# A decoder layer pair on one Trainium2 core: the last step of the norms on GpSimd, the expert tiles' PSUM copies on ScalarE, the last batch's gathers issued together

## What is computed

```
layer 0:  x = norm(x + decay_scan(x) @ o_w.T)             norm 0
          x = norm(x + cross_attention(x, ctx))           norm 1
          x = norm(x + fp4_gated_mlp(x))                  norm 2
layer 1:  h = norm(x) * gamma + beta                      norm 3
          a = x + linear_attention(h) @ wo
          h = norm(a) * gamma + beta                      norm 4
          x = norm(gelu(gelu(h @ w1 + b1) @ w2 + b2) + a + x)   norm 5
          x = norm(x + cross_attention(x, ctx))           norm 6
          x = norm(x + sum over 2 of 8 experts of gate * expert(x))
```

## Time and profile before

| what | value |
|---|---|
| median of 3 runs (lowest to highest) | 1092.96 us (1092.56 to 1093.59) |
| profiled execution, its own time | 1095.46 us |
| profiled execution, span of its instructions | 1093.6 us |
| busy: PE, DVE, ACT, POOL | 931.4, 681.5, 404.2, 253.5 us |
| mean granted clock of PE over the span | 0.917 |

### The profile page before, as it was taken

The page is one execution under the profiler, slowest core; times in us unless marked ns, Lnnn a source line. Parts: engine busy times, 40 slices in busy tenths (PEclk is TensorE's granted clock), DMA queues, the critical chain, the costliest instruction groups (busy, mean ns, idle before and its releaser), DMA issues.

```text
span 1093.6 us, 19946 instructions
## 1 busy us (share of the span) xinstructions
PE 931.4 (85%) x7490; PEld 734.6 (67%) x7490; DVE 681.5 (62%) x1995; ACT 404.2 (37%) x965; POOL 253.5 (23%) x384
## 2 busy tenths in 40 slices
PE   6579899888879999888999999989999997478940
PEld 4455578665655777666867887868778886367940
DVE  6997962559687543888785465784875365533124
ACT  2354334342532334433533544435343443112310
POOL 5410320115212210251221111340121112321025
PEclk9696999888888999988999999999999998599975
DMA  9996000000000000013210213314211031599912
GB/s 329 372 328 205 1 11 20 11 21 30 11 1 1 10 21 11 26 35 122 88 63 25 83 29 128 122 50 149 98 63 51 24 102 54 196 326 320 359 61 86
DMA packets 40734, 110.51 MB, mean 101 GB/s; under 512 B 5464, under 2 KB 25568, under 8 KB 39904
## 3 DMA queue, kind: packets, MB, share of 16 engines
q1 hardware_dynamic: 37568, 100.85, 27.2%
q0 software_dynamic: 3072, 8.39, 2.4%
HBM read 96.90 MB, written 35.13 MB: 121 GB/s over the span
## 4 chain that ended last, share of the span: by engine, by line
PE 60%; DVE 22%; issue 5%; DMA 5%; ACT 4%; POOL 2%; SPq 0%; POOLq 0%; DVEq 0%; ACTq 0%
PE ps L624 42%; PE ps L629 7%; PE ps L636 6%; DMA G<-ys_d,back_idx 3%; PE ps L700 2%; DVE PT L1021 2%; DVE stat L954 1%; ACT PT L1344 1%; DMA EW<-ys_d,back_idx 1%; PE ps L767 1%; DVE PT L974 1%; DVE sm L970 1%; DVE PT L979 1%; DVE X L1269 1%; POOL mv L1496 1%
## 5 line engine op out<-in xcount | busy, mean ns | idle before, releaser
L1496 POOL TENSOR_TENSOR stat<-stat,mhalf 128x1 f32<-128x1 f32 x112 | 66.2, 591 | 453.8 <-DVE stat L956 453.8
L624 PE MATMUL ps<-wall,XT 128*128 128x256 f32 (+1 forms) x448 | 137.2, 434 | 9.4 <-ACT XT L1311 4.3
L624 PEld LDWEIGHTS ps<-wall,XT 128*128 128x128 f32 x448 | 82.0, 199 | 36.5 <-issue 18.3
L636 PE MATMUL ps<-KB 32*128 32x128 f32 (+1 forms) x2048 | 81.1, 297 | 20.7 <-ACT PT L1344 4.9
L636 PEld LDWEIGHTS ps<-KB 32*128 32x128 f32 (+1 forms) x2048 | 68.5, 198 | 39.4 <-issue 28.9
L1021 DVE TENSOR_REDUCE PT<-ps 128x8 f32<-128x1024 f32 x64 | 75.3, 1219 | 26.8 <-PE ps L636 26.8
L624 PE MATMUL ps<-wgu,XT 128*128 128x352 f32 x256 | 85.1, 487 | 0.6 <-ACT XT L1311 0.6
L629 PE MATMUL ps<-cst,PT 128*128 128x128 f32 x512 | 79.0, 295 | 7.6 <-DVE PT L1012 4.6
L624 PE MATMUL ps<-XT,wall 128*128 128x128 f32 x640 | 77.1, 276 | 1.7 <-ACT XT L1361 1.5
L624 PEld LDWEIGHTS ps<-XT,wall 128*128 128x128 f32 x640 | 74.6, 192 | 5.6 <-ACT XT L1361 2.8
L629 PEld LDWEIGHTS ps<-cst,PT 128*128 128x128 f32 x512 | 62.7, 151 | 20.6 <-issue 10.1
(11 more groups left out here) (215 smaller groups left out, 1741.6 us busy)
## 6 DMA issues: line engine op xcount, KB each, us to landing
EW<-moe_w SPq DMA_DIRECT2D x31, 514.0 KB, 3.8
EW<-moe_w SPq DMA_DIRECT2D x31, 512.0 KB
PT<-moe_w SPq DMA_DIRECT2D x12, 514.0 KB, 5.9
PT<-moe_w SPq DMA_DIRECT2D x12, 512.0 KB, 7.1
XS<-xs_d SPq DMA_DIRECT2D x35, 128.0 KB, 2.4
ys_d<-YB SPq DMA_DIRECT2D x35, 128.0 KB, 3.9
wall<-wts SPq DMA_DIRECT2D x1, 4104.0 KB, 21.4
Y<-xTg SPq DMA_DIRECT2D x16, 128.0 KB, 2.2
```

The lines of the kernel that those rows point to most:

```text
L624: last = k.e.matmul(o, a, b, start=(i == 0), stop=(i == len(pairs) - 1))
L636: last = k.e.matmul(ps[:, at, c * P:(c + 1) * P], lhsT[lane, c * P:(c + 1) * P], rhs[lane, c * P:(c + 1) * P], start=True, stop=True)
L1496: return k.e.tensor_tensor(v[:, 7:8], v[:, 8:9], mhalf[:, :], ALU.pow)
```

## The change

1. The last step of norms 0 to 6 is taken from DVE. A new `pool_apply` on POOL does the same subtraction and multiplication behind the root that POOL makes itself; it still waits on `root_ready` and raises `normed`. In the plan the step costs POOL 0.65 where it cost DVE 0.41. The finish of the join (line 1275) stays on DVE.
2. Both copies from PSUM of an expert tile are taken from DVE and put on ACT, in all 46 tiles; `dve_tiles` is gone. In the plan each costs ACT 0.37 where it cost DVE 0.43.
3. In the last batch all eight "fetch" pieces, 16 gathers, come before the first join; before, three did.

With the changed costs the plan is made anew, so the interleaving on all engines and the banks can differ.

```diff
+APPLY = 0.65
@@ plan_attention
-    yield piece(work=[*[("s", 0.5, None)] * load, ("D", 0.41, (n, "done", a))])
+    yield piece(work=[*[("s", 0.5, None)] * load, ("P", APPLY, (n, "done", a))])
@@ plan_sample (and so for every norm)
-    yield piece(work=[("D", 1.27, None), ("P", 0.66, None)])
-    yield piece(work=[("D", 0.41, None)])
+    yield piece(work=[("P", APPLY, None), ("D", 0.87, None), ("P", 0.66, None)])
+    yield piece(work=[("P", APPLY, None)])
@@ plan_tiles
-            yield piece(0.3, [xT], [("D", 0.43, xT)], [("rows", x)], True)
+            yield piece(0.3, [xT], [("A", 0.37, xT)], [("rows", x)], True)
...
-            yield piece(1.78, [y], [("D", 0.43, y)],
+            yield piece(1.78, [y], [("A", 0.37, y)],
@@ join_turns
-        first = 3 if samples is BATCHES[-1] else 1
+        first = len(samples) if samples is BATCHES[-1] else 1
@@ dve_norm is gone, and its calls; dve_tiles is gone
@@ act_tiles
+                if what == "turn":
+                    act_copy(k, M["xT", x], XST[x % 2][:, :, :])
+                elif what == "down":
+                    u, i, y = M["y", x], home["store", x], user["store", x]
+                    k.wait_ge(filled[u.at], u.full)
+                    if y is not None:
+                        k.wait_ge(ys_stored[i], count["store", y])
+                    k.e.copy(YB[i][:, :], ps[:, u.at, 0:D]).then_inc(emptied[u.at], 1)
@@ pool
+        def pool_apply(k, n, ln, src, dst):
+            s = slot(n)
+            v = stat[:, s, :]
+            k.wait_ge(root_ready[s], norm_count(n, ln))
+            k.e.tensor_scalar(dst, src, v[:, 6:7], v[:, 7:8], ALU.subtract, ALU.mult).then_inc(normed[s], 1)
@@ pool_sample, pool_attention: one call behind each pool_norm, in the piece after it; for example
+            pool_apply(k, n, 2, Z[:, s, :], XB[:, s, :])
             e.memset(V1(s)[:, :, P:P + 1], 1.0)
             pool_norm(k, n, 3)
             yield
+            pool_apply(k, n, 3, XB[:, s, :], Y[:, s, :])
```

More of the change, by code:

```diff
@@ L180, in plan_sample @@
     yield piece(0.92, [(n, "o1")], [("D", 0.41, (n, "o1")), ("D", 0.87, None), ("P", 0.57, None)])
-    yield piece(work=[("p", 0.72, (n, "twice")), ("D", 0.41, None)])
+    yield piece(work=[("P", APPLY, None), ("p", 0.72, (n, "twice"))])
     load = n + NS < B
@@ L959, in dve_norm_stats @@
             dve_stats(k, stat[:, s, :], src, eps).then_inc(var_ready[s], 1)
[L961 to L965, removed]
         def dve_fp4_head(k, src, n, tmp, small, xn_sem):
@@ L984, in dve_fp4_scale, with dve_attention @@
                                      bc(small(1)[:, 0:m].unsqueeze(2), m, DH), ALU.mult)
-        def dve_attention(k, n, a, X, rope, xout):
+        def dve_attention(k, n, a, X, rope):
             e, s, u_ = k.e, slot(n), U[n]
@@ L1041, in dve_attention @@
             yield
-            dve_norm(k, n, (1, 6)[a], Z[:, s, :], xout)
             yield
@@ L1064, in dve_sample @@
             yield
-            dve_norm(k, n, 0, Z[:, s, :], XB[:, s, :])
             yield
-            yield from dve_attention(k, n, 0, XB, True, XA[:, s, :])
+            yield from dve_attention(k, n, 0, XB, True)
             k.wait_ge(normed[s], norm_count(n, 1))
@@ L1096, in dve_sample @@
             yield
-            dve_norm(k, n, 2, Z[:, s, :], XB[:, s, :])
             k.wait_ge(normed[s], norm_count(n, 2))
@@ L1100, in dve_sample @@
             yield
-            dve_norm(k, n, 3, XB[:, s, :], Y[:, s, :])
             yield
@@ L1132, in dve_sample @@
             yield
-            dve_norm(k, n, 4, XA[:, s, :], Y[:, s, :])
             yield
@@ L1146, in dve_sample @@
             yield
-            dve_norm(k, n, 5, Z[:, s, :], XA[:, s, :])
             yield
-            yield from dve_attention(k, n, 1, XA, False, X6[:, n, :])
+            yield from dve_attention(k, n, 1, XA, False)
         def dve_weights(k):
@@ L1275, in dve_join @@
                     e.tensor_scalar(x6, x6, v[:, 6:7], v[:, 7:8], ALU.subtract, ALU.mult).then_inc(out_ready, 1)
[L1276 to L1290, removed]
                 yield
@@ L1479, in act_tiles @@
             for what, x in tile_turns():
-                if what == "up":
+                if what == "turn":
[6 more added lines that the diff above has]
+                    k.e.copy(YB[i][:, :], ps[:, u.at, 0:D]).then_inc(emptied[u.at], 1)
+                elif what == "up":
                     u, i = M["h", x], home["load up", x]
@@ L1501, in pool_norm, with pool_attention @@
             pool_root(k, stat[:, s, :]).then_inc(root_ready[s], 1)
-        def pool_attention(k, n, a, X, rope):
+        def pool_apply(k, n, ln, src, dst):
[3 more added lines that the diff above has]
+            k.e.tensor_scalar(dst, src, v[:, 6:7], v[:, 7:8], ALU.subtract, ALU.mult).then_inc(normed[s], 1)
+        def pool_attention(k, n, a, X, rope, xout):
             e, s, u_ = k.e, slot(n), U[n]
@@ L1533, in pool_attention @@
             yield
+            pool_apply(k, n, (1, 6)[a], Z[:, s, :], xout)
             yield
@@ L1544, in pool_sample @@
             yield
+            pool_apply(k, n, 0, Z[:, s, :], XB[:, s, :])
             yield
-            yield from pool_attention(k, n, 0, XB, True)
+            yield from pool_attention(k, n, 0, XB, True, XA[:, s, :])
             yield
@@ L1573, in pool_sample @@
             yield
+            pool_apply(k, n, 4, XA[:, s, :], Y[:, s, :])
             u = u_["o1"]
@@ L1583, in pool_sample @@
             yield
+            pool_apply(k, n, 5, Z[:, s, :], XA[:, s, :])
             yield
-            yield from pool_attention(k, n, 1, XA, False)
+            yield from pool_attention(k, n, 1, XA, False, X6[:, n, :])
         def pool_weights(k):
@@ L1793, in _ @@
             dve_start(k)
-            in_order("D", [*slots_of(k, dve_sample), dve_weights(k), dve_router(k), dve_bias(k), dve_join(k), dve_tiles(k)])
+            in_order("D", [*slots_of(k, dve_sample), dve_weights(k), dve_router(k), dve_bias(k), dve_join(k), idle()])
         @block.scalar
```

## The result

The changed kernel took 1101.2 us as the median of six runs (1098.7 to 1104.4), against 1092.2 as the median of six of the kernel before. The ratio is 1.0093, with a 95% interval from 1.0064 to 1.0122: slower by 7 to 13 us. The forecast was 1080.5 with a range of 1067 to 1092.

The account below looks back on a forecast made before the run. PE was taken as the first limit, DVE second. Tiles -10, norms -4 and tail +1.3 gave -12.7 us: profiled 1095.5 to 1082.8, less 2.5 for the median 1080.3, given as 1080.5; range 1067 to 1092.

Parts of the forecast that it names:

- the loss bound: Norms' worst case: seven norms in four rounds, each 0.24 us later, 28 times 0.24 = 7, taken as a loss of 8.
- the one of the norms: Norms' step on POOL at 0.65 us: gain 4 us, ends a gain of 10 and a loss of 8.
- Rival (c): Norm rounds: POOL serialises four slots; up to 61 us lost, 31 at half exposed, 15 at a quarter; chance 0.10.
- the mark of 14: Sign in the norms: PE's transposes waiting above 14 us in total for POOL's apply would speak for POOL serialising the slots.
- DVE's relief: In the norms: 10.3 of PE's 14.0 us of waits for DVE's step come back once DVE is freer.
- The collisions of POOL and DVE: Shared SBUF ports: 112 applies meet some 16 DVE operations with two SBUF inputs, 0.4 us each, 6 us of DVE.
- The tiles: Batch 1's expert tiles: copies on ACT no longer wait behind joins on DVE, gaining 10 us, ends 4 and 13.
- The backlog behind the loads: End of batch 1's tiles: PE runs 12.6 us past its loads; never held, it would end one tile, 3.5 to 4 us, behind.
- rival (a): Tile stretch: transfers and SP hold it, PE waiting for loads (sign: above 8 us) instead of copies; about 1088; chance 0.20.
- rival (d): Whole kernel: the new order interleaves worse and takes the gains back, 1093, and nothing in the trace can show it; chance 0.08.
- The tail: Behind the last tile: 16 gathers at 1.25 us, then root 8, then joins at 2.11 us; 1.3 us longer.
- Rival (e): Behind the last tile: roots free to pass the gathers, tail 6 us shorter, time 1073; chance 0.03.

Follow-up runs that it names:

- q1: The changed kernel with the norms' POOL step in other forms (constants, root alone, one operation) for norms 3, 4 and 6; 1097.2 us in a single run.
- n2: The changed kernel with the norms' last step back on DVE, tile copies on ACT and gathers first kept; 1081.9 us, ratio 0.9867 to the kernel before.
- run 24: Not a follow-up run: the words are "Over the whole run 24 of the 112 roots", where 24 counts roots starting more than 0.5 us late.
- r2: The kernel before with the norms' last step on POOL, every order of its plan kept; 1110.8 us, ratio 1.0134 to the kernel before.
- a1: The kernel before with only the copies of the expert tiles moved to ACT; 1079.4 us, ratio 0.9873 to the kernel before.
- o1: The kernel before, same instructions and engines, its plan told 0.65 instead of 0.41 for the norms' step on DVE; 1089.2 us, ratio 0.9957.
- d1: The changed kernel, orders kept, with the norms' POOL step cut to one constant, 0.87 us for 1.23; 1091.4 us, ratio 0.9981 to before.
- p1: The changed kernel with its plan told 1.25 instead of 0.65 for the norms' step on POOL; 1097.1 us, ratio 1.0038 to the kernel before.
- n1: The kernel before with only the norms' last step moved to POOL, planned anew at 0.65; 1124.3 us, ratio 1.0293 to the kernel before.

## Why the prediction was wrong

**The price of the step is what failed.** The prediction bounded `tensor_scalar` on POOL by two-input operations of half and full width, 0.52 and 0.78 us, and took 0.65, since "this one has one tensor to read". It takes 1.23. The reasoning went by how much is read; q1 shows that the number of operations and of per-token operands counts too, and that the floor is at 0.87, above the upper bound. The rows of POOL held nothing with two operations in one instruction, so nothing made 0.78 an upper end, and the text used it as one. Carried into the loss bound, 1.23 would have given 28 x 0.82 = 23 us instead of 7, and the sum would have come out near zero or on the slow side. So the term that failed is the one of the norms: a gain of 4 us, from 10.3 of relief less 6 for the longer step and POOL's queue. In its place n2 shows a loss of 25 us (19 to 30).

The Trainium skill, as cited there (GPSIMD Engine Reference, When to use GPSIMD), was right in advising against the move and wrong in the half that promised relief: one-input work is near line rate, it says, and the prediction read that as 0.4 to 0.5 us. The runs show 0.87 to 1.23, and the measurement decides.

**Rival (c) came nearest, but not for its reason.** It had a chance of 0.10 and the right sign. It took the step at 0.65 us and had four slots wait for each other in POOL's queue. Norm 1 of the first four samples in the kernel after, with the end of each variance on DVE beside it, shows how far that goes:

```profile
85.83 0.15 DVE L958 TENSOR_SCALAR stat<-stat 128x1 f32<-128x1 f32 x1
86.07 0.56 POOL L1479 TENSOR_TENSOR stat<-stat,mhalf 128x1 f32<-128x1 f32 x1 [3.70 <-DVE stat L958]
86.73 1.23 POOL L1490 TENSOR_SCALAR XA<-Z,stat 128x256 f32<-128x256 f32 x1
87.05 0.15 DVE L958 TENSOR_SCALAR stat<-stat 128x1 f32<-128x1 f32 x1
87.93 0.78 POOL L1479 TENSOR_TENSOR stat<-stat,mhalf 128x1 f32<-128x1 f32 x1
88.81 1.23 POOL L1490 TENSOR_SCALAR XA<-Z,stat 128x256 f32<-128x256 f32 x1
89.92 0.15 DVE L958 TENSOR_SCALAR stat<-stat 128x1 f32<-128x1 f32 x1
90.16 0.56 POOL L1479 TENSOR_TENSOR stat<-stat,mhalf 128x1 f32<-128x1 f32 x1
90.83 1.23 POOL L1490 TENSOR_SCALAR XA<-Z,stat 128x256 f32<-128x256 f32 x1
91.14 0.15 DVE L958 TENSOR_SCALAR stat<-stat 128x1 f32<-128x1 f32 x1
92.02 0.56 POOL L1479 TENSOR_TENSOR stat<-stat,mhalf 128x1 f32<-128x1 f32 x1
92.69 1.49 POOL L1490 TENSOR_SCALAR XA<-Z,stat 128x256 f32<-128x256 f32 x1
```

POOL works here almost without a break from 86.07 to 94.18, 2 us for each slot. But the four don't arrive together. The first and the third root start within 0.1 us of their variances; the second and the fourth wait 0.7 us behind the step ahead of them. Over the whole run 24 of the 112 roots start more than 0.5 us late, the worst 3.1 us, where one did before. By the table above the queue ahead of the roots grew by 30 us over four slots, 8 us for one, where this rival's smallest case had 15; the step's length, 0.82 us for each of a slot's 28 norms, is 23. So the argument against the rival, that POOL idles 454 us waiting for variances, was half right (the idle time before the roots is still 360 us in the kernel after), and the price of the step did more than the queue.

What neither the forecast nor the rival had named is what else stands in the queue. PE's waits for POOL in the kernel after, by what it waited for:

```profile
PE ps L769 <- POOL KB L1549: 19.1, 6, 6.9
...
PE ps L631 <- POOL Y L1490: 5.9, 7, 2.0
PE ps L631 <- POOL XB L1490: 5.1, 6, 1.6
PE ps L631 <- POOL X L1490: 3.2, 6, 1.0
PE ps L631 <- POOL XA L1490: 1.1, 1, 1.1
```

For the step itself PE waits 15.3 us, just above the mark of 14 that was set for this rival; but it had waited 14.0 for DVE's step before, so the mark said little. More, 19.1 us (4.1 before), is for line 1549, the scaling of the quantised hidden rows, an instruction of 0.8 us that the change didn't touch and that stands behind roots and steps. At 138.29 PE has idled 6.92 us for it, though the scaling's input, which DVE made (the first row), was ready 3.5 us before the scaling began:

```profile
133.38 0.53 DVE L975 SCALAR_TENSOR_TENSOR PT<-PT 128x352 f32<-128x352 f32 x1
...
136.92 0.56 POOL L1479 TENSOR_TENSOR stat<-stat,mhalf 128x1 f32<-128x1 f32 x1 [1.79 <-DVE stat L958]
137.45 0.79 POOL L1549 TENSOR_TENSOR KB<-PT,sm 128x352 f32<-128x352 f32 x1
```
```profile
138.29 1.54 PE L769 MATMUL ps<-cst,KB 128*128 128x128 f32 x6 [6.92 <-POOL KB L1549]
```

The root ahead of it belongs to norm 3, whose statistics on DVE wait for norm 2's step on POOL (DVE waits for that step 12.5 us in eight places). So POOL waits for DVE, DVE waited for POOL, and the scaling waits for both. Summed over its 32 instructions the scaling starts 35 us after its input in the kernel after and 3 us in the kernel before.

**DVE's relief** was to give back 10.3 us. What it gives can't be read alone, since the step goes with it; r2 lost 15 us net of all relief, and by the table above its norms spend only 24 us less in DVE's queue, in four slots together, against 89 for the longer step. The collisions of POOL and DVE, put at 6 us of DVE, were no large item: the DVE instructions that both kernels have sum to 2 us more in the kernel after. Nor does show that two SBUF inputs are the condition of a collision, since the instruction that was held up there reads one tensor.

**The tiles.** The mechanism was right: in the tile stretch of the kernel after PE waits for no DVE instruction, and no longer the 9.1 us for XST. The size was off, 5.9 us instead of 10. The backlog behind the loads was to shrink to one tile, but the transfers are quiet only from 1050 us on (share 0.15) and PE goes on to about 1058.5, so 8 us remain of 12.6. PE now waits 16.3 us for row loads (6.8 before), above the 8 that were set as the sign of rival (a), and SP waits 16.4 us for eight finishes ahead of the stores of joined samples, as it did before (13.5); loads stand behind them.

```profile
PE ps L631 <- DMA XS<-xs_d: 16.3, 4, 6.6
```
```profile
SPq L1705 <- DVE X L1265: 16.4, 8, 3.1
```

So the clock did not stay near 1.00 from 950 us on either. In this row (stretch, PE busy, clock, DMA share, GB/s) PE works 45.8 of 59 us at 0.83:

```profile
951.00:1010.00 59.00, 45.80 (x293) 0.83 0.91 325
```

The halves of (a) and of the forecast are both in the result. The copies on ACT in the mixed stretch were costed at nothing, and neither a1 nor n2 shows a loss there; what a new order does by itself could hide a few us. What the prediction had at zero is the interleaving ahead of the tiles; o1 shows it at 9 us there, and it may be in a1's 10.7. That was rival (d), only considered as a loss and called invisible.

**The tail** was right in each step: gathers at 1.26 us, the first root behind the last of them, joins at 2.1 us, 36.9 us in all. Rival (e) is out.

How much of the error is the price? By d1, a step of 0.87 in place of 1.23 gains 12 us in the changed kernel, 33 us per us of step. From 1.23 to the assumed 0.65 that is 19 us (12 to 27), and 1101 - 19 = 1082, close to the forecast. It is an extrapolation beyond the shortest step that ran, and that it meets the forecast is in part luck, since the tiles gave 4 us less than forecast and the order has a few us of its own. What stays open is how the 25 us of the norms divide between the step's length and the plan in the changed kernel. p1 says 6 for the plan's wrong cost, but every new plan brings some 5 us of its own. One thing that a plan moves can be counted, ACT's table loads: 31 in the changed kernel, 34 in n1, 25 in a1 and n2, 23 in p1, 21 in before, o1 and r2. The two slowest plans have the most of them; that they are a cause was not tested.

## What to carry to other kernels

A price for an operation that an engine's rows don't show has no upper end in rows of simpler operations: measure it alone, or leave the range open and let the sign follow. An engine with idle time on average can still hold others up: look in the timeline at every innocent instruction that will stand behind the new ones, and at every pair of steps that now crosses between two engines. Ahead of "issue all transfers at once" ask which instruction of the issuing engine others wait for; in this tail nothing was gained until the waiting steps were moved behind the joins, and then 5 us.

## What had not been expected of the hardware and the schedule

- GpSimd's `tensor_scalar` on 128x256 float32 took 0.87 us with one constant and one operation, 0.93 with one per-token operand, 1.07 with two constants and 1.22 with two per-token operands; its two-input addition of that width took 0.72 to 0.79, and DVE's step with both operands 0.41.
- A gather of 128 rows held POOL's queue 0.96 us with 0.30 between two of them; sixteen of them held a root, and behind it DVE for 10.3 us.
- A fixed order made by a planner moved the time of identical instructions by 5 us (o1), and by about 17 us where it was made with half the true cost of a frequent step (n1 against r2).
- The order alone also set how often ACT loaded its function tables, at 1.28 us each: 21 times in r2 and 34 in n1, with the same work on ACT.
